# Convolution and GRU on one core: weights loaded first, the early convolution moved into step 1

## The chip, the core and the metric

One core of a Trainium2 chip runs the kernel. The time is device time in microseconds for one execution, the median of several runs. TensorE multiplies, VectorE, ScalarE and GpSimd do the elementwise work, SyncE only issues transfers; ScalarE and GpSimd issue some too. All engines run their own instruction lists and wait for each other through semaphores.

## What is computed

```python
# x (128, 64, 512), cond (128, 512), b (512), W_ih, W_hh (512, 1536), b_ih, b_hh (1536)
y = x + causal_depthwise_conv(x, taps=cond) + b      # 128 taps over 64 steps: lags 0 to 63 count
h = cond                                             # (batch 128, 512)
for t in range(64):
    gi, gh = y[:, t] @ W_ih + b_ih, h @ W_hh + b_hh
    r, z = sigmoid(gi_r + gh_r), sigmoid(gi_z + gh_z)
    n = tanh(gi_n + r * gh_n)
    h = (1 - z) * n + z * h
    out[:, t] = y[:, t] + h
```

## The kernel before

The batch has 128 rows, the channels four blocks of 128 (KB = 4). Every matrix product is made of three: each operand is split into a high part (rounded to fp32r) and a low part (the rest), and high x high, high x low and low x high are added in PSUM (block_product, L1077). A gate's product over the four channel blocks is thus 12 matmuls of 512 columns, and a step has six such groups: three gates of w_hh on h, three of w_ih on the convolved input of the next step, whose transposed form is xT.

The convolution is made in two parts. The **early** one gives steps 0 to 15 (EARLY = 16): x_early, a load of the first 16 inputs, times toep_early, the taps spread out by eight instructions (four on ScalarE, L655, four on VectorE, L862) from tap_blocks, which comes by way of the DRAM tensor tap_pad. It is 64 products into three PSUM banks (L1066 to L1075), whose 16 results VectorE evicts (L872) and SyncE stores to the DRAM tensor early, from which the xT of steps 1 to 15 are loaded (load_early_xT, L403). In the kernel before it is made before step 0. Step 0's own xT is made directly, from one row of x transposed on TensorE, times the tap of lag 0 plus the bias (L661 to L665).

The **late** (bulk) convolution gives steps 16 to 63: 128 banks of four matmuls (bulk, L1088), ten banks a step at ten points between the groups of steps 1 to 13 (POINTS, BULK_FIRST, BULK_LAST; bulk_bank, L325). Each needs a block of x_unit (loads of 256 KB in runs of 128 bytes, L418) split into high and low parts by ScalarE and VectorE (split), the taps' ring toep_ring (L429), and two evicting instructions (first_half on ScalarE, second_half on VectorE); the results go to the DRAM tensor xres, from which the xT of the later steps come.

From step FIRST_PAIR = 18 on, the w_ih products of two steps are made together with seven instead of eight half products (L1135, L1196 to L1258), with sums of inputs from GpSimd and combinations of the weights.

The order at the start is that of the instruction lists. SyncE (L372 to L407): tap_rows, h0, x_row, x_early, the twelve loads of w_ih, four biases broadcast to all partitions, then w_hh, then the stores of the early results, the xT of step 1, x_unit and toep_ring. ScalarE (L621 to L697): tap_pad, tap_blocks, bias_d and bias_pair issued, x_row reordered, k_full (the transposed taps), hT_hi, k_parts, its spread taps, xT of step 0, kernel_parts stored, the high parts of w_ih, the biases put into PSUM (put_bias), the high parts of w_hh. VectorE (L841 to L883): the low parts (low_weights, L352) in turns with the evictions, GpSimd those of the last channel block (on_pool). TensorE opens the PSUM banks of the gates with a matmul (L1053), makes the early convolution, then step 0.

## Time and profile before

| | us |
|---|---|
| median of 3 runs | 1177.78 (1176.2 to 1178.16) |
| profiled execution, its own time | 1179.38 |
| its span, first to last instruction | 1177.5 |
| TensorE busy (matmul) | 1135.4 (96%) |
| VectorE busy | 690.0 (59%) |
| ScalarE busy | 506.3 (43%) |
| GpSimd busy | 145.7 (12%) |

TensorE is busy in 96% of the span. It is the engine to follow: where it idles, the trace says which instruction of which engine released it. The page's slices show it idle in the first one above all. The other engines have room on average, but the average mixes stages: the start, steps with late convolution, and the paired steps.

### The profile page before, as it was taken

Reading aid. Unit: us, or ns where it says so; the run is one execution under the profiler, and the core shown is the slowest. Engines: PE = TensorE matmul, PEld = TensorE weight load, DVE = VectorE, ACT = ScalarE, POOL = GpSimd, SP = SyncE. Lnnn points to the kernel's source line nnn. Section 1 sums busy time; section 2 is a strip of 40 time slices with the busy share of each in tenths; the row PEclk is TensorE's granted clock in tenths of the full one; section 3 lists DMA queues with packets and bytes.
Section 4 is the critical chain, followed back from the end, with each engine's and each line's share of the span. In section 5 each row is a group of like instructions: output and inputs, shape, how many; then the busy total and the mean of one; then the engine's idle time right before and its main releaser. Section 6 shows DMA issues by size and latency. Waiting matters only on the chain.

```text
span 1177.5 us, 16672 instructions
## 1 busy us (share of the span) xinstructions
PE 1135.4 (96%) x5796; PEld 960.1 (82%) x5796; DVE 690.0 (59%) x1026; ACT 506.3 (43%) x965; POOL 145.7 (12%) x175
## 2 busy tenths in 40 slices
PE   1999999999999999999999999999999999999997
PEld 1977887878888888888888888888888888888885
DVE  2746775766775375555555655655555555655554
ACT  4527776767775343333323233333333333233332
POOL 0320010001001421111111000111111111100110
PEclk9999999999999999999999999999999999999999
DMA  9988888888863601110111111011111011111001
GB/s 247 286 193 167 160 172 165 173 174 171 174 151 91 147 18 37 36 35 25 31 36 36 36 36 28 25 36 36 36 36 27 27 36 36 36 36 32 26 23 27
DMA packets 284008, 96.97 MB, mean 82 GB/s; under 512 B 212688, under 2 KB 275664, under 8 KB 281920
## 3 DMA queue, kind: packets, MB, share of 16 engines
q1 hardware_dynamic: 278208, 91.83, 34.0%
q0 software_dynamic: 1664, 3.41, 0.9%
q10 hardware_dynamic: 4096, 1.22, 0.4%
q8 instruction: 23, 0.38, 0.1%
q14 instruction: 17, 0.14, 0.0%
HBM read 62.26 MB, written 34.14 MB: 82 GB/s over the span
## 4 chain that ended last, share of the span: by engine, by line
PE 92%; SPq 2%; ACT 1%; DMA 1%; DVE 1%; issue 1%; ACTq 0%; DVEq 0%
PE bank L1081 40%; PE sum_a L1140 17%; PE sum_c L1140 12%; PE bank L1174 7%; PE bank L1178 4%; PE sum_c L1081 3%; PE sum_a L1105 3%; PE bank L1043 2%; PE sum_a L1070 2%; PE sum_c L1105 1%; SPq L422 1%; PE sum_c L1070 1%; DMA early<-early_result 1%; SPq L435 1%; ACT toep_early L655 0%
## 5 line engine op out<-in xcount | busy, mean ns | idle before, releaser
L1081 PE MATMUL bank<-w_hh_hi,hT_hi 128*128 128x512 f32 x584 | 232.3, 398 | 0.1
L1081 PE MATMUL bank<-w_hh_lo,hT_hi 128*128 128x512 f32 x584 | 228.4, 391 | 0.0
L1081 PE MATMUL bank<-w_hh_hi,hT_lo 128*128 128x512 f32 x584 | 227.8, 390 | 0.0
L783 ACT ACTIVATE n_gate<-q 128x512 f32<-128x512 f32 x64 | 40.5, 633 | 249.2 <-DVE q L984 249.2
L1081 PEld LDWEIGHTS bank<-w_hh_hi,hT_lo 128*128 128x128 f32 x584 | 109.9, 188 | 23.9
L1081 PEld LDWEIGHTS bank<-w_hh_hi,hT_hi 128*128 128x128 f32 x584 | 109.9, 188 | 22.4 <-DVE hT_lo L838 0.5
L1081 PEld LDWEIGHTS bank<-w_hh_lo,hT_hi 128*128 128x128 f32 x584 | 110.3, 189 | 17.8
L823 ACT ACTIVATE hT_hi<-bank 128x512 fp32r<-128x512 f32 x63 | 37.6, 597 | 140.1 <-PE bank L1043 140.1
L838 DVE TENSOR_TENSOR hT_lo<-bank,hT_hi 128x512 fp32r<-128x512 f32 x64 | 44.1, 689 | 87.4 <-ACT hT_hi L823 87.0
L596 POOL TENSOR_TENSOR x_sum<-xT 128x256 f32<-128x256 f32 x23 | 17.3, 752 | 628.2 <-DMA xT<-xres 628.1
L889 DVE TENSOR_TENSOR x_parts<-x_unit,x_parts 128x512 fp32r<-128x512 f32 x64 | 70.5, 1102 | 39.0 <-ACT x_parts L706 38.8
L772 ACT ACTIVATE r<-bank 128x512 f32<-128x512 f32 x64 | 38.2, 597 | 119.2 <-PE bank L1178 113.0
L996 DVE TENSOR_TENSOR q<-z,q 128x512 f32<-128x512 f32 x64 | 45.4, 709 | 75.3 <-ACT z L802 74.9
L974 DVE TENSOR_TENSOR q<-bank,r 128x512 f32<-128x512 f32 x64 | 44.1, 688 | 63.5 <-PE bank L1081 62.2
L706 ACT ACTIVATE x_parts<-x_unit 128x512 fp32r<-128x512 f32 x64 | 73.7, 1152 | 17.5 <-PE sum_a L1105 8.2
L987 DVE TENSOR_TENSOR q<-h,n_gate 128x512 f32<-128x512 f32 x64 | 54.2, 847 | 35.7 <-ACT n_gate L783 35.7
L1174 PE MATMUL bank<-w_hh_hi,hT_hi 128*128 128x512 f32 x184 | 72.1, 392 | 0.8 <-ACT hT_hi L823 0.8
L1174 PE MATMUL bank<-w_hh_lo,hT_hi 128*128 128x512 f32 x184 | 71.6, 389 | 0.0
L716 ACT ACTIVATE tmp<-sum_a,bias_pair 96x128 f32<-96x128 f32 x172 | 52.0, 355 | 23.5 <-PE sum_a L1105 22.9
L551 POOL DMA_DIRECT2D out_dram<-outZ x52 | 28.4, 553 | 263.0 <-DVE outZ L1032 262.7
L1081 PE MATMUL bank<-w_ih_hi,xT_hi 128*128 128x512 f32 x144 | 60.1, 417 | 0.0
L1105 PEld LDWEIGHTS sum_a<-x_parts,toep_ring 128*96 128x96 f32 x344 | 44.9, 163 | 17.9 <-issue 5.3
(153 smaller groups left out, 2375.2 us busy)
## 6 DMA issues: line engine op xcount, KB each, us to landing
x_unit<-in_x_dram SPq DMA_DIRECT2D x64, 256.0 KB, 4.6
out_dram<-outZ SPq DMA_DIRECT2D x204, 64.0 KB, 1.6
toep_ring<-kernel_parts SPq DMA_DIRECT2D x128, 96.0 KB, 3.2
xres<-stage SPq DMA_DIRECT2D x32, 384.0 KB, 4.8
xT<-xres SPq DMA_DIRECT2D x192, 64.0 KB, 1.9
early<-early_result SPq DMA_DIRECT2D x4, 1024.0 KB, 13.6
xT<-early SPq DMA_DIRECT2D x60, 64.0 KB, 2.1
out_dram<-outZ POOLq DMA_DIRECT2D x52, 64.0 KB, 3.0
```

What stands on the lines that cost most here:

```text
L706: nc.scalar.activation(part_block(j, 0), x_block(j), ACT.Copy).then_inc(x_hi_ready, 1)
L716: nc.scalar.activation(tmp[m % 2][0:2 * LATE, pair * B:(pair + 1) * B], conv_bank[m % 3][0:2 * LATE, pair * 2 * B:pair * 2 * B + B], ACT.I ...
L838: nc.vector.tensor_tensor(lo_out[:, :], full[:, :], hi_in[:, :].bitcast(F32), ALU.subtract).then_inc(lo_ready, 1)
L889: nc.vector.tensor_tensor(part_block(j, 1), x_block(j), part_block(j, 0).bitcast(F32), ALU.subtract).then_inc(x_lo_ready, 1)
L974: nc.vector.tensor_tensor(q[:, :], ps_hn[:, :], r[:, :], ALU.mult).then_inc(reset_h_ready, 1)
L987: nc.vector.tensor_tensor(gate_in_order(q), in_order(h), gate_in_order(n_gate), ALU.subtract).then_inc(h_less_n_ready, 1)
L996: nc.vector.tensor_tensor(q[:, :], z[:, :], q[:, :], ALU.mult).then_inc(z_part_ready, 1)
L1081: mm = nc.tensor.matmul(psum[:, :], a[:, rows], b[w][:, cols], start=False, stop=stop and n == 2, skip_group_check=True)
L1105: mm = nc.tensor.matmul(conv_bank[m % 3][0:2 * LATE, pair * 2 * B:pair * 2 * B + cols], late, parts[j % HL_RING][:, slot * 2 * B:slot * 2 ...
L1140: mm = nc.tensor.matmul(total[:, at], stationary, cols, start=opens and k == 0 and n == 0, stop=k == 1 and n == 2, skip_group_check=True)
L1174: nc.tensor.matmul(ps_r[:, :], hT_hi[:, k * P:(k + 1) * P], part[1][:, w_cols(k, R)], start=False, stop=False, skip_group_check=True)
L1178: mm = nc.tensor.matmul(ps_r[:, :], hT_lo[:, k * P:(k + 1) * P], hi[1][:, w_cols(k, R)], start=False, stop=k == KB - 1, skip_group_check=True)
```

## The change

- POINTS is 12, and the late convolution uses 11 of them: 11 banks a step in steps 3 to 14 (BULK_OF).
- SyncE loads tap_rows, h0, then w_hh and w_ih. x_early (it lies where x_rows and the taps lie now) is loaded after everything that reads those is done. The early results go out in eight stores from three tiles.
- The early convolution is made in step 1, two banks at each of the points 2 to 9 (early_banks, early_products).
- x of steps 0 to 3 is made directly: x_rows, four loads from ScalarE's queue in runs of 128 bytes, 16 transposes on TensorE (transpose_x), the tap of lag 0 and the bias on ScalarE (y_base), the other lags by 24 multiply-adds of 128 columns on VectorE (y_sums). The loads from the DRAM tensor early begin with step 4.
- The biases are loaded as rows and brought into PSUM by four matmuls with a tile of ones; ScalarE copies them to SBUF.
- Four spread_taps move from ScalarE to GpSimd, between its low parts; VectorE's four stand between its low parts too. bias_d and bias_pair are issued by GpSimd.
- In step 0 TensorE makes the w_hh products first, each as its low parts come, then those of w_ih (first_step_products). The high parts' order is w_hh R, N, Z, w_ih R, N, Z.
- Pairs start at step 20 instead of 18; the loads and combinations around it move a step on.

The core of the diff:

```diff
-POINTS = 10
-BULK_FIRST, BULK_LAST = 1, 13
+POINTS = 12
+DIRECT = 4
+EARLY_STEP, EARLY_POINT = 1, 2
+BULK_FIRST, BULK_LAST = 3, 14
-    QUARTERS = 4
+    RESULTS = 8
+    RESULT_TILES = 3
-    FIRST_PAIR = EARLY + 2
+    FIRST_PAIR = EARLY + 4
...
-        GATES = ((R, Z, N), (R, N, Z))
-        W_PARTS = [(w, k, g) for w in range(2) for g in GATES[w] for k in range(KB)]
+        GATES = ((R, N, Z), (R, N, Z))
+        W_PARTS = [(w, k, g) for w in (1, 0) for g in GATES[w] for k in range(KB)]
...
+            load_weights(1, w_hh)
             load_weights(0, w_ih)
...
+            sp.wait_ge(tap_pad_stored, 16 * 2)
+            sp.wait_ge(k_parts_stored, 16 * QUADS)
...
+            sp.wait_ge(y_base_ready, KB * DIRECT)
+            sp.wait_ge(y_sum_ready, Y_SUMS[-1])
+            for b4 in range(4):
+                bs = slice(b4 * B // 4, (b4 + 1) * B // 4)
+                sp.dma_start(
+                    x_early[:, :].rearrange("p (b g) -> p b g", g=G0)[:, bs],
+                    x[bs, 0:EARLY, :].rearrange("b s (c g) -> (s c) b g", g=G0),
+                ).then_inc(x_early_loaded, 16)
...
+            for n in range(RESULTS):
+                sp.wait_ge(early_evicted, (n + 1) * NB0 // RESULTS)
...
+                sp.wait_ge(early_stored[n], 16 * len(range(n, RESULTS, RESULT_TILES)))
+            for t in (DIRECT, DIRECT + 1):
+                sp.wait_ge(outT_ready, t - RING + 1)
+                load_early_xT(t)
...
+                if isinstance(t, int) and t == BULK_LAST:
+                    store_stage(NBANK * 2 // STAGE - 1)
+                    for n in range(2):
+                        sp.wait_ge(stage_stored[n], 32 * (PAIRS // STAGE // 2))
+                    sp.wait_ge(outT_ready, BULK_LAST)
+                    for late in range(EARLY, BULK_LAST + RING):
+                        load_xT(late % RING, T - 1 - late)
...
+            for q4 in range(QUADS):
+                pool.dma_start(bias_d[q4 * QUAD:(q4 + 1) * QUAD, :],
...
+            low_parts(1, R)
+            pool.wait_ge(tap_blocks_loaded, 16)
+            pool.wait_ge(in_block_set, 1)
+            spread_taps(0)
+            low_parts(1, N)
+            spread_taps(1)
+            low_parts(1, Z)
+            spread_taps(2)
+            low_parts(0, R)
+            spread_taps(3)
+            low_parts(0, N)
+            low_parts(0, Z)
...
+            store_early_out(0)
+            pool.wait_ge(early_done, NB0)
+            nc.gpsimd.memset(toep_ring[:, :].bitcast(F32), 0.0).then_inc(toep_cleared, 1)
+
+            for t in range(1, BULK_LAST):
+                store_early_out(t)
...
+            act.dma_start(b_rows[0:1, :], b_ih.unsqueeze(0)).then_inc(bias_loaded, 16)
+            act.dma_start(b_rows[1:2, 0:N], b_hh[0:N].unsqueeze(0)).then_inc(bias_loaded, 16)
+            act.dma_start(b_hn_row[:, :], b_hh[N:NG].unsqueeze(0)).then_inc(bias_loaded, 16)
+            for k in range(KB):
+                act.dma_start(
+                    x_rows[:, k * D:(k + 1) * D].rearrange("b (t q r) -> b (t q) r", q=QUADS, r=QUAD),
+                    x[:, 0:DIRECT, :].rearrange("b t (q k r) -> b k (t q) r", q=QUADS, k=KB)[:, k],
+                ).then_inc(x_rows_loaded, 16)
...
+            act.wait_ge(banks_opened, 1)
+            for tile, psum in ((bias_rz[:, R:R + D], ps_r), (bias_hn[:, :], ps_hn), (bias_rz[:, Z:Z + D], ps_z),
+                               (bias_in[:, :], ps_in)):
+                nc.scalar.activation(tile, psum[:, :], ACT.Copy).then_inc(biases_kept, 1)
+            act.wait_ge(tap_pad_stored, 16 * 2)
+            act.dma_start(tap_blocks[:, :].rearrange("p (u g) -> p u g", g=G0),
+                          bass.AP(tap_pad.tensor, tap_pad.offset, [[G0, P], [D, EARLY], [1, G0]])
+                          ).then_inc(tap_blocks_loaded, 16)
...
+            def y_base(t):
+                act.wait_ge(x_rows_done, t + 1)
+                for k in range(KB):
+                    nc.scalar.activation(xT[t][:, k * P:(k + 1) * P], ps_x[t][:, k * P:(k + 1) * P], ACT.Identity,
+                                         bias=bias_d[:, k:k + 1],
+                                         scale=k_full[:, k * P + T - 1:k * P + T]).then_inc(y_base_ready, 1)
+
+            high_weights(1, R)
+            act.wait_ge(bias_early_done, 1)
+            nc.scalar.activation(bias_early[:, :], ps_hT[:, 0:G0], ACT.Copy).then_inc(bias_early_ready, 1)
+            high_weights(1, N)
+            act.wait_ge(conv_bias_loaded, 16 * (QUADS + 2))
+            y_base(0)
+            act.wait_ge(y_base_ready, KB)
+            nc.scalar.activation(xT_hi[:, :], xT[0][:, :], ACT.Copy).then_inc(xT_hi_ready, 1)
+            high_weights(1, Z)
+            y_base(1)
+            y_base(2)
+            high_weights(0, R)
+            y_base(3)
+            high_weights(0, N)
+            high_weights(0, Z)
...
+                if not isinstance(i, bass.RuntimeValue) and t == 0:
+                    act.wait_ge(y_sum_ready, Y_SUMS[1])
+                    nc.scalar.activation(xT_hi[:, :], xT[1][:, :], ACT.Copy).then_inc(xT_hi_ready, 1)
...
+            def y_sums(t):
+                for lag in range(1, t + 1):
+                    for k in range(KB):
+                        at = slice(k * P, (k + 1) * P)
+                        tap = k * P + T - 1 - lag
+                        nc.vector.scalar_tensor_tensor(xT[t][:, at], ps_x[t - lag][:, at], k_full[:, tap:tap + 1],
+                                                       xT[t][:, at], ALU.mult, ALU.add).then_inc(y_sum_ready, 1)
+            low_parts(1, R)
             dve.wait_ge(tap_blocks_loaded, 16)
+            spread_taps(4)
+            spread_taps(5)
+            low_parts(1, N)
             low_part(xT_lo, xT[0], xT_hi, xT_hi_ready, xT_lo_ready, 1)
+            spread_taps(6)
+            low_parts(1, Z)
+            y_sums(1)
+            spread_taps(7)
+            low_parts(0, R)
+            y_sums(2)
+            low_parts(0, N)
+            y_sums(3)
+            low_parts(0, Z)
...
+            pe.wait_ge(bias_loaded, 16 * 3)
+            pe.wait_ge(ones_set, 1)
+            for psum, rows, bias in ((ps_r, 2, b_rows[0:2, R:R + D]), (ps_z, 2, b_rows[0:2, Z:Z + D]),
+                                     (ps_in, 1, b_rows[0:1, N:NG]), (ps_hn, 1, b_hn_row[:, :])):
+                mm = nc.tensor.matmul(psum[:, :], ones[0:rows, :], bias, start=True, stop=True)
+            mm.then_inc(banks_opened, 1)
...
+            def early_products(n):
+                if n >= 3:
             ...
+                for slot in range(BANK // B):
+                    g = n * (BANK // B) + slot
+                    mm = nc.tensor.matmul(conv_bank[n % 3][:, slot * B:(slot + 1) * B],
+                                          toep_early[:, g * P:(g + 1) * P],
+                                          x_early[:, :].rearrange("p (b g) -> p g b", g=G0)[:, g, :],
+                                          start=True, stop=True)
+                mm.then_inc(early_done, 1)
...
+            def first_step_products():
+                for psum, gate in ((ps_r, R), (ps_hn, N), (ps_z, Z)):
+                    for k in range(KB):
+                        low_weights_ready(1, k, gate)
+                        block_product(psum, hT_hi, hT_lo, 1, gate, k, False)
+                    if gate == R:
+                        pe.wait_ge(x_rows_loaded, 16 * KB)
+                        for t in range(DIRECT - 1):
+                            transpose_x(t)
+                        pe.wait_ge(bias_early_ready, 1)
+                        transpose_x(DIRECT - 1)
+                pe.wait_ge(xT_lo_ready, 1)
+                for psum, gate, done in ((ps_r, R, gh_r_done), (ps_in, N, gh_n_done), (ps_z, Z, gh_z_done)):
+                    for k in range(KB):
+                        low_weights_ready(0, k, gate)
+                        mm = block_product(psum, xT_hi, xT_lo, 0, gate, k, k == KB - 1)
+                    mm.then_inc(done, 1)
...
+                            for n in early_banks(t, g * POINTS // GROUPS):
+                                early_products(n)
```

## Rows read from the trace of the kernel before

**Rows 1.** The page, first part: busy time, share, instructions of each engine
```profile
PE 1135.4 (96%) x5796; PEld 960.1 (82%) x5796; DVE 690.0 (59%) x1026; ACT 506.3 (43%) x965; POOL 145.7 (12%) x175
```
**Rows 2.** Stretches: length, busy time of PE, PEld, DVE, ACT, POOL, clock, DMA share, GB/s
```profile
0.00:29.50 29.50, 4.54 (x14) 3.11 (x15) 6.10 (x10) 11.86 (x15) 2.08 (x11) 1.00 0.94 247
...
29.50:82.70 53.20, 53.19 (x240) 47.43 (x241) 32.92 (x44) 22.12 (x39) 14.71 (x8) 1.00 0.96 247
82.70:105.00 22.30, 18.68 (x96) 14.34 (x95) 11.65 (x19) 14.06 (x28) 2.32 (x4) 1.00 0.83 159
...
105.00:368.00 263.00, 257.84 (x1387) 215.87 (x1386) 178.35 (x288) 188.99 (x408) 26.11 (x48) 0.99 0.78 163
```
**Rows 3.** TensorE's waits, 105 to 380 us: total, times, longest
```profile
PE sum_c L1105 <- issue: 2.7, 2, 1.9
```
**Rows 4.** The chain that ended last, by start and length, 0 to 130 us
```profile
9.67 2.96 ACTq L631
```
**Rows 5.** TensorE in order of time, 28 to 112 us: the first product after the convolution
```profile
57.55 0.59 PE L1081 MATMUL bank<-w_ih_hi,xT_hi 128*128 128x512 f32 x1
```
**Rows 6.** Stretches with weights' loads alone, and with x_unit's alone
```profile
30.00:35.00 5.00, 5.00 (x25) 4.86 (x24) 3.27 (x5) 3.79 (x9) 0.00 (x0) 1.00 1.07 229
...
70.00:74.00 4.00, 4.00 (x19) 3.34 (x18) 2.01 (x3) 3.04 (x5) 0.00 (x0) 1.00 1.08 172
```
**Rows 7.** SyncE's issues of two tiles: nanoseconds min/median/max, first and last start
```profile
L385 SPq DMA_DIRECT2D w_ih_raw<-in_L_cond_W_ih_dram x12: 426/432/4763, 16.2 to 25.8; - x12
...
L422 SPq DMA_DIRECT2D x_unit<-in_x_dram x64: 617/1258/2707, 67.8 to 321.0; - x64
```
**Rows 8.** ScalarE in order of time: table load, xT pieces, high parts
```profile
15.12 1.28 ACT L640 ACT_TABLE_LOAD   x1 [15.12 <-issue]
...
27.92 1.45 ACT L662 ACTIVATE xT<-sum_c,bias_d,k_full 128x128 f32<-128x128 f32 x4
...
46.41 2.18 ACT L683 ACTIVATE w_hh_hi<-w_hh_raw 128x512 fp32r<-128x512 f32 x4
```
**Rows 9.** DMA issues, 0 to 110 us: count, KB each, median us to landing
```profile
tap_blocks<-tap_pad ACTq DMA_DIRECT2D x1, 512.0 KB, 5.2
...
kernel_parts<-k_parts ACTq DMA_DIRECT2D x4, 128.0 KB, 10.0
```
**Rows 10.** DMA queues (q1 SyncE's, q10 ScalarE's), 12:14 us, then 36:41: packets, MB, share
```profile
q10 hardware_dynamic: 1967, 0.50, 110.2%
q1 hardware_dynamic: 99, 0.10, 16.4%
...
q1 hardware_dynamic: 593, 1.54, 77.3%
q10 hardware_dynamic: 526, 0.47, 27.5%
```
**Rows 11.** Spread taps, GpSimd's 1024-column add, and VectorE's low parts of w_ih
```profile
18.78 3.89 DVE L862 TENSOR_SCALAR toep_early<-tap_blocks,in_block 128x1024 f32<-128x1024 f32 x4
...
41.90 2.38 POOL L540 TENSOR_TENSOR bias_rz<-bias_rz,bias_tmp 128x1024 f32<-128x1024 f32 x1 [38.89 <-DMA bias_hn<-in_L_cond_b_hh_dram]
...
L354 DVE TENSOR_TENSOR w_ih_lo<-w_ih_raw,w_ih_hi x9: 681/682/2067, 32.2 to 50.0; 128x512 fp32r<-128x512 f32 x9
```
**Rows 12.** Chain rows of 512-column matmuls at both levels; a stretch with its clock
```profile
18.21 0.86 PE bank L1054 x2
...
382.65 2.73 PE sum_c L1081 x12
...
184.00:188.00 4.00, 4.00 (x18) 3.42 (x17) 1.88 (x4) 2.52 (x6) 0.00 (x0) 0.71 0.85 172
```
**Rows 13.** VectorE's transposes that end steps 19 and 63
```profile
475.22 0.71 DVE L1032 STREAM_TRANSPOSE outZ<-outT 128x512 f32<-128x512 f32 x1
...
1173.19 0.71 DVE L1032 STREAM_TRANSPOSE outZ<-outT 128x512 f32<-128x512 f32 x1
```
**Rows 14.** GpSimd's stores of step 3's output: four issues, and the pause before
```profile
152.72 2.17 POOL L551 DMA_DIRECT2D out_dram<-outZ  x4 [19.15 <-DVE outZ L1032]
```

More of the change, by code:

```diff
@@ L136, in conv_residual_gru @@
     toep_early = place("toep_early", G0 * P)
-    quarter = [None] * QUARTERS
-    for n in reversed(range(QUARTERS)):
-        quarter[n] = place(f"early_result{n}", G0 // QUARTERS * B)
-    assert top[0] <= gru_end
+    result = [place(f"early_result{n}", G0 // RESULTS * B) for n in range(RESULT_TILES)]
+    assert top[0] <= outT_at
     top[0] = x_at
@@ L171, in conv_residual_gru @@
     lag0_row = place("lag0_row", 8, parts=EARLY)
-    bias_tmp = place("bias_tmp", N)
-    assert top[0] <= w_at["hh"] + KB * NG * KW
-    top[0] = w_at["hh"] + KB * NG * KW
-    x_row, h0 = place("x_row", D), place("h0", D)
+    h0 = place("h0", D)
+    ones = place("ones", P, parts=2)
+    b_hn_row = place("b_hn_row", D, parts=1)
+    assert top[0] <= toep_at
+    top[0] = bias_first_at
+    b_rows = place("b_rows", NG, parts=2)
+    assert top[0] <= bias_first_at + 2 * NCOL * KW
+    top[0] = outZ_at
+    tap_blocks = place("tap_blocks", EARLY * G0)
+    assert top[0] <= outZ_at + 2 * D * KW
     ctx = ExitStack()
@@ L183, in conv_residual_gru @@
         ps_in = sum_c[:, BANK:2 * BANK]
-        ps_x0 = conv_bank[2]
+        ps_x = [*conv_bank, ps_hT]
         def sem(name):
@@ L767, in step @@
                 first_half(bulk_bank(t, 0))
-                if not isinstance(i, bass.RuntimeValue) and t == 0:
-                    for n in range(QUARTERS):
-                        act.wait_ge(early_stored[n], 16)
                 act.wait_ge(gh_r_done, t + 1)
@@ L945, in step @@
                     x_first_low(0, u + 1)
-                    for n in range(2, NCOMBO):
-                        combo_low(n)
                 if odd and follows:
@@ L993, in step @@
                     sums_low(slice(D, 2 * D), sum34_hi_ready, sum34_lo_ready, j + 1)
+                if not isinstance(i, bass.RuntimeValue) and t == 0:
+                    low_part(xT_lo, xT[1], xT_hi, xT_hi_ready, xT_lo_ready, 2)
+                split(split_block(t, 4))
+                second_half(bulk_bank(t, 4))
+                early_evicts(t, 4)
                 dve.wait_ge(h_less_n_ready, t + 1)
@@ L1052, in _, with transpose_x @@
+            mm.then_inc(banks_opened, 1)
+            def transpose_x(t):
+                for k in range(KB):
+                    mm = nc.tensor.transpose(ps_x[t][:, k * P:(k + 1) * P],
+                                             x_rows[:, k * D + t * P:k * D + (t + 1) * P], ident[:, :])
+                mm.then_inc(x_rows_done, 1)
             pe.wait_ge(hT_hi_ready, 1)
-            for psum in (ps_r, ps_z, ps_in, ps_hn):
-                mm = nc.tensor.matmul(psum[:, :], hT_hi[:, 0:P], hT_hi[:, :], start=True, stop=True)
```

320 lines of the change are left out of this document (140 added, 180 removed).

## The prediction

> **What bounds the kernel now.** The shares of the span come first: TensorE is busy for 1135.4 of 1177.5 us, so only the 42 us in which it is not, and the work that it is given, can move the time [rows 1]. Then the stretches: TensorE idles 25.0 us of the first 29.5, then runs to 82.7 us without a gap (early convolution, all gates of step 0, w_ih products of step 1); it idles 3.6 us to 105 us, while the late convolution starts, and 5.2 us from there to 368 us [rows 2]. The waits put these last down to "issue" at the late convolution's matmuls, 1.9 us the longest [rows 3]. The chain of waits shows what fills the first 29 us: ScalarE's queue is stuck for 2.96 us issuing behind a transfer [rows 4], and its spread taps and the pieces of xT follow.
>
> So the sum is made on TensorE: when its continuous work starts, how far the first step stretches, and what is lost later. Its reference is the start of step 1 at 82.7 us plus the 3.6 us lost in that step, 86.3 us, with the early convolution done. In the new kernel that convolution, the 28.0 us from 29.5 to 57.55 [rows 5], falls into step 1.
>
> **ScalarE's queue up to the first weights (T0).** Three bias rows at 0.43 us, as the issue of any unblocked load [rows 7], from 0.8 us on give 2.1 us. The four x_rows loads have 2048 runs of 128 bytes each, as x_unit's loads have. Those move 172 GB/s, 1.5 us for 256 KB, and hold their issuer for a median 1.26 us; a weights' load, over 32 partitions, gets 229 GB/s, 1.14 us for 256 KB [rows 6, 7]. SyncE now issues 24 of those from 1.7 us on. If the two queues take turns, four x_rows loads take 4 x (1.5 + 1.14) = 10.6 us, and ScalarE is stuck behind them as it was behind tap_blocks: free at 13, after three small issues at 14.2 us (9 if nothing blocks, 17 if more weights slip in). Table load 1.3, k_full, hT_hi and k_parts three at 0.5, four bias copies at 0.55: 19.2 us [rows 8]. The four openings by a row of ones, now plain f32, have no row; the nearest are the old ones at 0.43 us each [rows 12]. Even at four times that they end by 13 us and cost nothing; without that cover, up to 7 us. Then tap_blocks' issue 0.4, the block behind it 3.0, kernel_parts' four 1.7: T0 = 24.3 us, between 18.5 and 32.
>
> **tap_blocks' landing (L).** It used to have no weights ahead of it and landed in 5.2 us; kernel_parts, 512 packets issued among weights' loads, took 10.0 us [rows 9]. While both hardware queues had work, at 36 to 41 us, they moved 593 and 526 packets: one for one, whatever their size [rows 10]. Taken one for one with weights' packets, tap_blocks' 2048 would land only once all weights have: 24 x 1.14 + 4 x 1.5 + 1.8 for tap_blocks + 4 for start and landing = 39 us. So L is between 19 (issued at 14 us, if nothing blocks, and 5.2 on) and 39. I take 31: 10.0 us from 19.5 would be 29.5, and this has four times the packets.
> The Trainium skill (DMA: Bandwidth & Descriptors, "Queues, rings and completion order") says that each DMA engine goes round the queues that hold work, packet by packet. The equal counts of [rows 10] agree with it. By that rule alone L would be 39.
>
> **The first step's products (their end, F).** ScalarE: 24 high parts at 0.55 = 13.1, sixteen pieces of xT at 0.33 = 5.2, xT_hi and bias_early 0.9 [rows 8]: 19.3 us, and with 3.7 for the last low part and products T0 + 23. GpSimd: its four spread_taps have no row, and lie between VectorE's 1.0 and twice its own 2.38 for a 1024-column add, to which I set them; with six low parts at 1.2, half of it, that is 17 us and up [rows 11], beside ScalarE's. VectorE's order puts spread_taps(4) ahead of all but the first low parts, so from L on it owes four spreads 4.0, fifteen low parts at 0.68 = 10.2, xT_lo 0.7, and 24 adds of 128 columns. Those have no row; between a quarter of VectorE's 0.68 and ScalarE's 0.36 for that size I take 0.23: 5.5 us. That is 20.4, and 0.3 of the last product: 20.7. GpSimd works beside it, and low parts that did so went up to 2.07 us [rows 11]; I add 2 (0 to 6). F is the larger of 24.3 + 23 = 47.3 and 31 + 20.7 + 2 = 53.7: **53.7 us**, between 41.5 and 65. VectorE becomes the bound, behind a late transfer. The low parts used to be hidden by the early convolution; they stand bare now.
>
> **Clock.** TensorE works in bursts in that step. After a long pause two 512-column matmuls took 0.86 us, where twelve take 2.73: 0.43 and 0.23 each, the 1.2 and the 2.4 GHz level; after 1.7 us of waiting at 180 us the granted clock fell to 0.71 [rows 12]. A gate's group of 2.7 us would take 5.2, over a pitch of 3.5 to 4. From 0 to 4 us; I take 0, since VectorE is the later one.
>
> **The turn of the step.** After F come q's add, tanh, a bias copy, the xT_hi of step 1 and its xT_lo: 0.7 + 0.6 + 0.6 + 0.6 + 0.7, some 3.3 us of idle TensorE. Then x_r and x_n 5.4, transposes 0.4, x_z 2.7: step 1 begins at F + 11.9 = 65.6 us and, with 28.0 us of convolution, stands at 93.6 where the old kernel stood at 86.3: **+7.3 us**. The x_early load waits for the last adds (F - 2) and moves 4.19 MB, 17 us at the first stretch's 247 GB/s [rows 2], less as it then runs alone; it is wanted six groups of 0.68 us into step 1, at F + 16. That is 0 to 1 us, I take 0; past that cover each us costs one. The 16 evictions lie beside 44 us of TensorE.
>
> **Pairs.** FIRST_PAIR goes from 18 to 20, so one pair of steps is made directly: 2 x (6 x 2.73 + 0.4) = 33.6 us [rows 12] against 2 x (1173.19 - 475.22) / 44 = 31.7 us [rows 13]: **+1.9 us**.
>
> **Late convolution.** 128 banks go from 13 steps of ten to 12 of eleven; TensorE's work is the same. A step of ten took 19.15 + 2.17 = 21.3 us [rows 14], 4.5 more than one without. Eleven will take 21.75 us, 1.98 a bank for 2.13, so its DMA share of 0.78 [rows 2] becomes 0.84. The stalls of 5.2 us at a bank can grow with it, and the 3.6 us at the start can recur in step 3. 0 to 5 us more; I take **+2.3**. The combined low parts after h move one step on, where TensorE has products of w_ih to cover them. GpSimd's six loads at the start, some 0.55 us each [rows 14], delay k_zeroed to about 7 us; ScalarE wants it at 15. The 12 added transposes, 1.3 us, fit into TensorE's gaps. The xT loads of steps 16 and 17 go ahead of the store and have 8 us of cover.
>
> **Sum.** 7.3 + 1.9 + 2.3 = +11.5 us. The profiled execution took 1179.38 us around its span of 1177.5, 1.6 above the median 1177.78: 1190.9 against itself, **1189.3** against the median.
>
> **Rivals.**
> *Starved queue*: weights win the packets, L = 39, F = 61.7: 8 us more, 1197 us; with VectorE slowed fully 1201. For it: the one-for-one counts. Against: at 12 to 14 us tap_blocks moved 1967 packets to the other queue's 99 [rows 10], so that queue could run dry while tap_blocks was taken in.
> *Free queues* (the other side): the x_rows issues don't block ScalarE, which is free at 9 us; T0 = 18.5, L = 19 to 21, F = 41.5 to 44.5. Step 1 stands 4.9 to 1.9 us ahead, and with the pair's 1.9 that is 1174.8 to 1177.8; if the late convolution, begun two steps later, loses half of its 8.8 us less, down to 1170. It decides at F = 44.5: below that, faster. For it: w_ih's loads were issued at 0.43 us, faster than they moved. Against: x_unit's 1.26.
> *The late convolution binds*: eight more waits of 2 us, 16 in place of 2.3: 1203 us. For it: waits of up to 1.9 us at ten banks a step. Against: only some five in 128 banks.
>
> **How the numbers follow.** Forecast 0.47 (its own range 1182 to 1195), starved 0.17, late convolution 0.08, free 0.28. Of the last, 0.18 lies more than 0.2% below (2.4 us, about what a measurement here can tell) and 0.10 within it; slower is 0.72. The range leaves out the far ends of the free and the late-convolution case: 1174 to 1202.
>
> **What would show it.** ScalarE's first high part of w_hh at 24 us (18.5: free; over 30: starved). tap_blocks landing at 31 with VectorE's spread right behind. Step 0's last w_ih product ending at 54, TensorE idle for 3 us after it, step 1 from 66 us on for 45 us. Over 14 us of waits at late banks would prove the third rival. The prediction is wrong at the root if TensorE's products in step 0 follow each other without gaps, or if x_early is what step 1 waits for.

## The result, and the profile after

The changed kernel takes **1225.8 us** (median of 4 runs, 1222.0 to 1226.9) where the kernel before, run beside it, takes 1177.0: a ratio of 1.041 (1.038 to 1.044), 48.8 us more. Forecast were 1189.3 us, 1174 to 1202. The direction was right, and two of the three terms of the sum were far too small. The profiled execution has a span of 1223.5 us, against 1177.5 before: +46.0 us, and this is what is split up below. One of e3's four runs took 1270.6 us at a granted clock of 0.85, where the others took 1192.7 to 1193.5 at 0.99; it is left out of e3's numbers.

The page of the changed kernel, its busy line (answers to [rows 1]):

```profile
PE 1154.9 (94%) x5800; PEld 965.5 (79%) x5800; DVE 694.8 (57%) x1041; ACT 500.8 (41%) x971; POOL 159.1 (13%) x185
```

TensorE is 19.5 us longer busy: its four openings by a row of ones take 7.6 us where the old ones took 2.4, twelve transposes and a directly made pair of steps came in, and more of its products run at the 1.2 GHz level (below: *cold* products). Its idle time grew from 42 to 69 us. The stretches say where (columns as in [rows 2]; the first two are that group's, the others follow the new kernel's course):

```profile
0.00:29.50 29.50, 8.21 (x12) 3.20 (x12) 1.10 (x3) 0.00 (x0) 5.94 (x18) 1.00 1.02 213
29.50:82.70 53.20, 31.88 (x115) 23.11 (x116) 33.39 (x56) 29.26 (x59) 26.13 (x10) 0.94 0.45 110
41.50:75.70 34.20, 25.58 (x88) 17.98 (x88) 30.12 (x50) 22.66 (x48) 26.13 (x10) 0.90 0.18 51
86.00:130.00 44.00, 44.00 (x202) 39.46 (x201) 16.08 (x24) 5.28 (x9) 4.34 (x5) 1.00 0.25 96
165.00:420.00 255.00, 239.78 (x1284) 196.96 (x1283) 167.89 (x274) 180.52 (x392) 24.05 (x44) 0.99 0.80 167
```

In the first stretch the DMA share is 1.02 and ScalarE (0.00) computes nothing at all. Where the old kernel filled 29.5 to 82.7 us with TensorE (53.19 of 53.20), the new one has 31.9 us of it and the DMA engines stand at 0.45. Step 1 with the early convolution (86 to 130 us) runs without a gap, as forecast. In the late part (165 to 420 us) 15.2 us of 255 are idle, at a DMA share of 0.80.

The chain that ended last, 0 to 78 us, by start, length and what:

```profile
1.88 0.41 ACTq L682
2.32 2.78 ACTq L682
5.13 9.92 ACTq L682
15.08 14.76 ACTq L682
29.88 5.41 ACTq L687
...
41.54 0.64 ACT w_hh_hi L722
42.20 0.70 DVE w_hh_lo L374
43.04 5.15 PE bank L1180 x12
48.20 0.45 PE sum_a L1147 x4
48.73 1.52 ACT xT L727 x4
50.27 0.64 ACT xT_hi L738
50.94 0.69 DVE xT_lo L889
51.63 1.88 DVE toep_early L911
53.52 1.72 DVE w_hh_lo L374 x3
...
62.30 3.15 DVE w_ih_lo L374 x3
...
70.55 5.09 PE bank L1180 x12
75.65 0.64 ACT xT_hi L855
```

ACTq L682 are the four x_rows issues: for 27.96 us ScalarE gets no further in its instruction list. L687 is tap_pad behind them. So T0, ScalarE's first w_hh high part, is 41.5 us and not 24.3. Behind it is a chain through four engines in turn: a low part, twelve products at the 1.2 GHz level (5.15 us; [rows 12] has 2.73 for twelve at 2.4), the transposes of x, ScalarE's pieces, and then VectorE without a pause from 50.9 to 70.5 us, and twelve cold products again (5.09 us). The end of step 0's products, F, is 75.6 us where 53.7 was forecast.

The DMA queues between 2 and 20 us (as in [rows 10]; q1 is SyncE's, q10 ScalarE's):

```profile
q1 hardware_dynamic: 1925, 3.50, 85.8%
q10 hardware_dynamic: 3129, 0.40, 18.3%
```

x_rows has 8192 packets of 128 bytes. In 18 us 3129 of ScalarE's went through, for 1925 of the weights', and the weights had the engines for 86% of the time. Both queues made progress, packet beside packet if not exactly one for one, but a packet of x_rows carries a sixteenth of what one of the weights' does. The last x_rows load landed at 36.7 us, the last of the weights at 35.0.

TensorE's waits from 130 to 420 us (total, times, longest), against [rows 3]:

```profile
PE sum_a L1204 <- issue: 8.0, 6, 2.2
PE sum_c L1204 <- issue: 5.3, 3, 2.5
PE sum_a L1204 <- DVE stage L986: 3.7, 4, 1.2
```

All are at products of late banks, 17.0 us; the third rival was to be proved by 14.

### The profile page after: what moved, and what is told of

Its sections match the earlier page's. It is cut to its first block, busy times and chain, and to the rows that moved or that the text cites. A ratio compares the mean times of both kernels' runs of the same rounds, so it can differ in the third digit from the quotient of the medians.

```text
span 1223.5 us, 16696 instructions
## 1 busy us (share of the span) xinstructions
PE 1154.9 (94%) x5800; PEld 965.5 (79%) x5800; DVE 694.8 (57%) x1041; ACT 500.8 (41%) x971; POOL 159.1 (13%) x185
## 3 DMA queue, kind: packets, MB, share of 16 engines
q1 hardware_dynamic: 275760, 88.95, 31.9%
## 4 chain that ended last, share of the span: by engine, by line
PE 83%; DVE 5%; ACT 4%; ACTq 3%; issue 2%; SPq 2%; DMA 0%; DVEq 0%
PE bank L1180 36%; PE sum_a L1251 15%; PE sum_c L1251 11%; PE bank L1289 7%; PE sum_c L1180 3%; PE bank L1293 3%; ACTq L682 2%; PE bank L1132 2%; PE sum_a L1204 2%; PE sum_a L1170 2%; ACT x_parts L754 2%; SPq L446 1%; PE sum_c L1204 1%; DVE x_parts L972 1%; ACT tmp L764 1%
## 5 line engine op out<-in xcount | busy, mean ns | idle before, releaser
L1180 PE MATMUL bank<-w_hh_hi,hT_lo 128*128 128x512 f32 x592 | 232.2, 392 | 0.0
L1180 PE MATMUL bank<-w_ih_hi,xT_hi 128*128 128x512 f32 x160 | 68.1, 426 | 4.3 <-POOL w_ih_lo L374 1.7
L1180 PE MATMUL bank<-w_ih_hi,xT_lo 128*128 128x512 f32 x160 | 63.4, 396 | 0.0
```

Source lines behind the costliest of these rows:

```text
L1180: mm = nc.tensor.matmul(psum[:, :], a[:, rows], b[w][:, cols], start=False, stop=stop and n == 2, skip_group_check=True)
```

## The experiments

Times in us. L is where tap_blocks landed (issue plus its time to landing), F the end of step 0's products, "x_unit" the start of the first and of the last x_unit load, ratio that to the kernel before with its 95% interval.

| kernel | T0 | L | F | x_unit | time | ratio |
|---|---|---|---|---|---|---|
| before | - | - | - | 67.8, 321.0 | 1177.0 | 1 |
| changed | 41.5 | 41.8 | 75.6 | 129.0, 380.3 | 1225.8 | 1.041 (1.038 to 1.044) |
| e1 | 27.1 | 38.6 | 69.1 | 122.5, 372.8 | 1213.8 | 1.030 (1.023 to 1.036) |
| e2 | 29.6 | 37.7 | 69.2 | 122.5, 374.2 | 1218.8 | 1.034 (1.030 to 1.038) |
| e8 | 24.0 | 24.3 | 58.4 | 111.7, 364.6 | 1209.1 | 1.027 (1.025 to 1.029) |
| e9 | 24.2 | 24.5 | 55.9 | 113.5, 365.1 | 1210.2 | 1.028 (1.026 to 1.030) |
| e12 | 23.5 | 23.8 | 56.9 | 112.4, 365.6 | 1210.1 | 1.027 (1.024 to 1.030) |
| e13 | 23.9 | 24.1 | 54.5 | 109.8, 359.5 | 1204.9 | 1.024 (1.022 to 1.025) |
| e3 | - | - | - | 67.2, 316.1 | 1193.0 | 1.012 (1.009 to 1.016) |
| e14 | - | - | - | 68.4, 327.9 | 1174.9 | 0.998 (0.997 to 0.999) |

e1, e2, e8, e12 and e13 have two runs each. Those of e1 lie 10.7 us apart (1208.4 and 1219.1), the others 1.6 to 2.5, so that a difference of 1 or 2 us between two of these kernels says nothing. e8 contains the edit of e2; e9 and e12 contain e8, and e13 contains e12.

**The start: what holds ScalarE, and tap_blocks.**

```diff
+            sp.wait_ge(x_rows_loaded, 16 * KB)
             load_weights(1, w_hh)
```

> The changed kernel, with one wait added on SyncE: the 24 weights' loads begin only when the four x_rows loads have landed. Theory A (ScalarE's queue is held up because its x_rows loads share the DMA engines with the weights): alone, the four loads of 256 KB in 128-byte runs need some 1.5 us each, ScalarE is past them by about 10 us instead of 29.8, its first w_hh high part comes at 18 to 20 us instead of 41.5, and the time falls by 15 to 20 us, to about 1208. Rival (the x_rows loads are slow of themselves, 7 us each for 2048 runs, weights or no weights): ScalarE is still stuck until about 28 us, the weights land 20 us later than before, the first high part stays at 40 us or later and the time is 1226 or more. Theory B (the chain from that high part to the end of the first step's products takes 34 us of itself): that distance stays 34 us in both cases.

ScalarE in order of time, 1 to 28 us (start, length, line, what):

```profile
1.88 5.68 ACTq L683 DMA_DIRECT2D x_rows<-in_x_dram  x4
...
13.42 0.43 ACTq L705 DMA_DIRECT2D tap_blocks<-tap_pad  x1
13.89 9.80 ACTq L710 DMA_DIRECT2D kernel_parts<-k_parts  x1
...
27.13 2.19 ACT L723 ACTIVATE w_hh_hi<-w_hh_raw 128x512 fp32r<-128x512 f32 x4 [11.65 <-issue]
```

Theory A holds for the cause and missed the sizes: alone, the four issues take 5.7 us, beside the weights 28. T0 came at 27.1, not 18 to 20, because the block moved on: one kernel_parts issue now stood 9.8 us behind tap_blocks, and tap_blocks, issued 25 us earlier than in the changed kernel, landed only 3 us earlier:

```profile
tap_blocks<-tap_pad ACTq DMA_DIRECT2D x1, 512.0 KB, 25.1
```

It landed at 38.6 us, while the last four of the 24 weights' loads were still under way (42.4 us for the last). Theory B failed here and in e2: from T0 to F it is 42.0 and 39.6 us, not 34, as VectorE now waits for tap_blocks; counted from L it is 30.5 and 31.5 us (33.8 in the changed kernel).

```diff
-                act.dma_start(x_rows[:, k * D:(k + 1) * D]..., x[:, 0:DIRECT, :]...)   # 128-byte runs
+                act.dma_start(x_plain[:, t * D:(t + 1) * D], x[:, t, :])               # 2 KB runs
```

> The changed kernel, with x of steps 0 to 3 loaded as four loads of whole 2 KB rows (512 runs in all in place of 8192) and put into the order of x_rows by four VectorE copies, some 0.7 us each. The weights still go out at the same time. If the two queues are served run for run (theory A in its strict form), 512 runs are through after as many of the weights' runs, and ScalarE is free by about 5 us: first w_hh high part at 19 us or when the weights have landed (w_hh r landed within 10 us), time about 1226 - 22 = 1204. Rival (the share goes by bytes, or the issue order does it, and the size of the runs does not matter): ScalarE free at 15 us or later, first high part at 27 us or more, time 1211 or more. Theory B: the chain from the first high part to the end of the step's products stays at 34 us.

```profile
1.88 1.81 ACTq L684 DMA_DIRECT2D x_plain<-in_x_dram  x4
...
14.04 1.28 ACT L692 ACT_TABLE_LOAD   x1 [14.04 <-POOL k_parts L574]
...
15.97 0.40 ACTq L703 DMA_DIRECT2D tap_blocks<-tap_pad  x1
...
17.29 8.98 ACTq L708 DMA_DIRECT2D kernel_parts<-k_parts  x1
```

With the same bytes in 512 packets the four issues take 1.81 us, so it is the number of packets that held the queue. ScalarE was free by 6.2 us and then waited until 14.0 for GpSimd's k_parts, which stood behind a bias_pair issue that came 7.1 us late (2.6 in e1, where the weights had not yet been issued): this, the weights' own landing and kernel_parts' issue put T0 at 29.6 and not 19, and the time at 1218.8 and not 1204. tap_blocks landed at 37.7 us, 21.7 us after its issue. The Trainium skill (DMA: Bandwidth & Descriptors, "Queues, rings and completion order") says that each DMA engine goes round the queues with work packet by packet. e2 agrees: tap_blocks landed 0.2 us behind the last of the weights (37.5 us), near the 39 us that the prediction had for turns of one to one; the counts above, 3129 to 1925, say that the turns are not exactly that.

```diff
             load_weights(1, w_hh)
+            sp.wait_ge(tap_blocks_loaded, 16)
             load_weights(0, w_ih)
```

> The kernel e2_x_rows_contiguous with one wait added: SyncE issues w_ih's twelve loads only when tap_blocks has landed. In e2 tap_blocks was issued at 15.9 us and landed 21.7 us later, at 37.7 us, with the last of the weights. Theory A' (tap_blocks' 2048 packets wait among the weights' packets): it now shares with the last of w_hh alone and lands 5 to 8 us after its issue, by 24 us; VectorE's spreads begin 13 us earlier, step 0's products end at 24 + 31 = 55 us in place of about 69, and the time falls by 10 to 14 us, to about 1206. It costs nothing unless w_ih, landed by 38 us, comes after ScalarE wants it. Rival (tap_blocks is slow of itself, its 128-byte runs out of a buffer just written): it lands after 38 us again, w_ih after 50 us, and the time is over 1230.

tap_blocks, 2048 packets of 256 bytes, landed 8.2 us after its issue, at 24.3 us, and F came at 58.4 for 69.2 (55 was expected): theory A' holds, and w_ih came in time. F gained 10.8 us, and the time 9.7, just under the 10 to 14 expected. Of the 48.8 us that the change costs, the two edits of e2 and e8 give back 17.

**The chain from T0 to F.** It took 34.1 us in the changed kernel, 34.4 in e8, where tap_blocks lands 0.3 us after T0 and so no longer holds it up.

```diff
-            spread_taps(0..3) on GpSimd, between its low parts
+            the same four on VectorE, behind low_parts(0, Z)
```

> The kernel e8_tap_blocks_before_w_ih with GpSimd's four spread_taps (4.4 to 5.1 us each in the changed kernel) made by VectorE behind its last low part. They are wanted in step 1 only. Theory B (GpSimd's spreads delay its own low parts, and slow VectorE's work beside them: two spreads took 2.9 us, three low parts 3.6): VectorE's spreads go to 1.0 us and its low parts to 0.68, TensorE waits for no low part of GpSimd, and the first step's products end 22 to 25 us after tap_blocks' landing in place of 31; time 5 to 8 us below e8, some 1199. A share of it can be lost at the start of step 1, as x_early's load, 12.2 us long, now goes out only after those four spreads. Rival (the chain is set by ScalarE's 24 high parts and 16 pieces and by TensorE's 1.2 GHz stretches): it stays at 29 us or more and the time within 2 us of e8.

F fell by 2.5 us, to 31 us behind L and not 22 to 25, and the time not at all. Theory B's numbers failed and the rival's came true, in part for another reason than the rival's: the spreads were wanted "in step 1 only", but they stood in VectorE's instruction list ahead of q, which the next step's input waits for, and TensorE waited 4.4 us for xT_lo behind them:

```profile
60.30 0.80 PE L1183 MATMUL bank<-w_ih_hi,xT_hi 128*128 128x512 f32 x1 [4.36 <-DVE xT_lo L883]
```

```diff
             def first_step_products():
+                transpose_x(0..2)
                 for psum, gate in ((ps_r, R), (ps_hn, N), (ps_z, Z)):
                     ...
-                    if gate == R: transpose_x(0..2)
```

> The kernel e8_tap_blocks_before_w_ih with TensorE's transposes of x of steps 0 to 2 put ahead of the first w_hh products, in place of behind the r gate's twelve. In e8 ScalarE stood waiting for them until 31.4 us, behind a group of products at 1.2 GHz (5.35 us), and VectorE for xT_lo from 32.1 to 33.6 us, with 20.7 us of its own work still to do. Theory (that detour is on the chain to the end of the first step): xT_lo comes about 2 us earlier, the end of step 0's products at 56 us in place of 58.4, and the time falls by 2 us, to 1207. Rival (ScalarE's order of high parts sets it): less than 0.7 us.

xT_lo came 2.0 us earlier (31.6 us), F 1.5 us, and the time stayed, so the theory failed on the time. The traces show where the 1.5 us went. Here are the twelve products behind F, then the next twelve, first in e8, then in e12:

```profile
59.81 3.01 PE bank L1186 x12
62.83 2.73 PE sum_c L1186 x12
```
```profile
58.91 4.34 PE bank L1186 x12
63.25 2.98 PE sum_c L1186 x12
```

e12 starts them 0.9 us earlier and ends them 0.7 us later, since they run at a granted clock of 0.77 (58.9 to 66.3 us) and those of e8 at 1.00. VectorE in e12, from 31.6 us on:

```profile
31.61 0.68 DVE L889 TENSOR_TENSOR xT_lo<-xT,xT_hi 128x512 fp32r<-128x512 f32 x1
...
39.24 3.76 DVE L376 TENSOR_TENSOR w_ih_lo<-w_ih_raw,w_ih_hi 128x512 fp32r<-128x512 f32 x3
...
52.12 2.98 DVE L376 TENSOR_TENSOR w_ih_lo<-w_ih_raw,w_ih_hi 128x512 fp32r<-128x512 f32 x3
```

Three low parts take 1.89 us when GpSimd is quiet (the last row below); in e12 it works all through, and they take up to 3.76. The last kernel of this line puts GpSimd's four spreads on ScalarE, behind its last high part:

```diff
             high_weights(0, Z)
+            for c in range(C0 // 2): nc.scalar.activation(toep_early_block(c), ..., scale=in_block[:, c:c + 1])
```

> The kernel e12_transposes_first with GpSimd's four spread_taps made by ScalarE behind its last high part, where it stood idle from 43.7 to 47.8 us; the old kernel paid 1.85 us for one there. In e12 VectorE worked without a pause from 31.6 to 54.9 us, 23.3 us, and in e9, where GpSimd had no spreads, the same work took 19.7 us; but e9 put four spreads of 0.96 us into VectorE's own queue behind it. Theory B (GpSimd's spreads slow VectorE's low parts beside them and hold back its own; e9 gave the gain back by its four spreads): VectorE's stretch is 19.7 us, step 0's products end at 53 to 54 us in place of 56.9, x_early's load goes out 3 us sooner, and the time falls by 3 us, to about 1206.5. Rival (the time of the changed kernel no longer hangs on the end of step 0, as the late convolution's supply takes the gain): under 1 us.

```profile
39.38 1.87 DVE L376 TENSOR_TENSOR w_ih_lo<-w_ih_raw,w_ih_hi 128x512 fp32r<-128x512 f32 x3
...
49.17 1.89 DVE L376 TENSOR_TENSOR w_ih_lo<-w_ih_raw,w_ih_hi 128x512 fp32r<-128x512 f32 x3
```

VectorE's stretch is 18.9 us (32.2 to 51.1) in place of 23.5, F 54.5 for 56.9, the time 5.2 us below e12: theory B holds, and 2 us more came than it said (the late part took 274.9 us from first to last product in place of 278; why, was not tried). What GpSimd's spreads cost VectorE is thus 4.6 us; what its low parts cost is still in the 18.9. The rest of the chain is the detour by the cold group and ScalarE, of which e12 took 2 us, and the cold group at its end, which no run took away.

e13 also shows what a good start alone is worth. Its step 1 begins at 66.7 us, where the prediction had 65.6, and still it takes 1204.9 us and not 1189.3. Of the 15.6 us between them 14.5 are lost behind that point.

**The late convolution.**

```diff
-POINTS = 10
-BULK_FIRST, BULK_LAST = 1, 13
+POINTS = 12
+BULK_FIRST, BULK_LAST = 1, 12
```

> The kernel before with one thing changed: the late convolution's 128 banks are spread over steps 1 to 12 with eleven a step, in place of steps 1 to 13 with ten. TensorE has the same products in all. Theory C (the late banks are bounded at about 2.18 us each by what feeds them, whatever stands around them): eleven banks make a step of 24.0 us, the last bank comes at the same time as before, but by then TensorE has done about 1.2 steps less of the gates, so the time grows by 12 to 18 us, to 1190 to 1195. Rival (the late part in the changed kernel was slow through its late start, not through eleven banks a step): a step takes 22.6 us and the time stays within 3 us of 1177.

The kernel before becomes 14.5 us slower (10 to 19) by this alone. Its start is untouched. From the first x_unit load to the last it is 248.9 us, and from the first late product to the last 276.1 us; in the changed kernel 276.3, in e13 274.9. That is 2.16 us a bank, whatever the start. Theory C holds.

```diff
             def load_x_part(unit, part):
+                if unit >= 2: return
```

> The changed kernel without the x_unit loads of units 2 to 7 (12.6 of 16.8 MB of x): the late convolution multiplies the first two units' x again and again. This leaves part of the loading out, so the output is not the reference's. Theory C1 (the supply of the late banks through the DMA engines and SyncE's queue is the bound, at 2.18 us a bank): steps 3 to 13 fall from 24.1 to the 22.6 us or less of TensorE's work, TensorE's idle time of 15 us between 165 and 420 us mostly goes, and the time falls by 13 to 17 us to about 1210. Rival C2 (the splits and evictions on ScalarE and VectorE, one bank behind, hold the banks): steps 3 to 13 stay at 24 us and the time at 1224 to 1226.

One run, 1205.0 us, with a span 20.7 us below the changed kernel's. Its stretch and TensorE's only waits from 105 to 400 us:

```profile
165.00:420.00 255.00, 254.42 (x1380) 212.49 (x1379) 176.21 (x289) 186.79 (x411) 26.85 (x48) 1.00 0.52 124
```
```profile
PE sum_a L1206 <- DVE stage L988: 1.1, 2, 0.9
```

ScalarE and VectorE still have all their splits and evictions, and TensorE is idle for 0.6 us. So it is the transfers (C1), not the crowding (C2). Not all that they cost shows as a wait. Here are the changed kernel and e4 from the first late product to the last, with the same 1386 products of TensorE:

```profile
149.00:425.50 276.50, 259.07 (x1386) 212.45 (x1386) 180.46 (x294) 194.37 (x422) 25.32 (x47) 0.99 0.79 163
```
```profile
149.90:405.00 255.10, 253.38 (x1386) 211.10 (x1386) 179.94 (x294) 193.00 (x423) 25.18 (x47) 1.00 0.54 127
```

Of the 21.4 us between them 15.7 are idle time; in 5.7 the same products take longer, in part because they are cold after a wait (granted clock 0.99 for 1.00). In e3 it is likewise: 16.5 us of waits at late banks for 8.6 in the kernel before, and TensorE busy for 1141.5 us in place of 1135.4.

GpSimd's stores show the length of a step of eleven without and with x_unit's traffic; the first fence is e4, the second the changed kernel:

```profile
218.00 2.17 POOL L603 DMA_DIRECT2D out_dram<-outZ  x4 [19.91 <-DVE outZ L1123]
239.85 2.17 POOL L603 DMA_DIRECT2D out_dram<-outZ  x4 [19.68 <-DVE outZ L1123]
```
```profile
196.21 2.19 POOL L601 DMA_DIRECT2D out_dram<-outZ  x4 [19.45 <-DVE outZ L1121]
222.22 2.18 POOL L601 DMA_DIRECT2D out_dram<-outZ  x4 [23.81 <-DVE outZ L1121]
```

21.9 us against 26.0 here, 24.2 in the mean of eleven steps (from the store at 148.1 us to that at 414.5). The 21.75 us of the prediction were TensorE's own time and right; they were not what counted.

Is it SyncE's single queue or the DMA engines behind it?

```diff
-                    load_toep(m // 2 + 3)        # SyncE
+                        load_toep_here(m // 2 + 3)   # GpSimd, as are the first ones
```

> The changed kernel with all loads of toep_ring issued by GpSimd, whose queue then holds them and the early outputs; SyncE keeps x_unit, xT and the stores of stage. From SyncE's first x_unit load to its last it is 253.2 us in the kernel before, 251.3 in the changed one, 248.9 with eleven banks a step: the late convolution takes 250 us however it is spread. Theory C1a (SyncE's single queue, in which each load is held up behind the one before it, sets that 250 us; the DMA engines are busy only 0.80 of the time): with the small loads in a queue of their own it falls to 240 us or less, TensorE's idle 15 us between 165 and 420 us mostly goes, and the time falls by 8 to 14 us, to about 1214. Rival C1b (the DMA engines' own work on 128-byte runs sets it): it stays at 250 us and the time within 3 us of 1226. Rival C1c (GpSimd issues a toep load more slowly than SyncE's 1 us and stands in the way of its own): longer than 253 us, time over 1230.

> The kernel before with the same edit: all loads of toep_ring issued by GpSimd. TensorE stands idle 5.2 us between 105 and 350 us there, and 3.6 us in step 1. Theory C1a: the waits at late banks go, 3 to 7 us less, some 1172. Rival C1b: within 2 us of 1177.5. Rival C1c: 5 us or more slower.

Both fell to the third case, and far beyond its number. e11 takes 1366.9 us (1.161, 1.158 to 1.164); e10's two timings lie far apart (1423.6 and 2918.1), its span is 1421.3. GpSimd's waits in e11, 105 to 540 us:

```profile
POOL toep_ring L549 <- issue: 317.5, 112, 5.7
```

An issue is 0.69 us, but the next one follows only some 3 us later, with nothing in the profile that it waits for. Why is not shown. So this told nothing on SyncE's queue against the DMA engines: that stays open.

The kernel before the other way round: 128 banks in steps 1 to 14, nine a step and ten in two, first combined pair at step 20.

```diff
-POINTS = 10
-BULK_FIRST, BULK_LAST = 1, 13
+POINTS = 11
+BULK_FIRST, BULK_LAST = 1, 14
+        TEN = (12, 13)
```

> The kernel before with its 128 late banks in steps 1 to 14, nine a step and ten in two of them, in place of ten in steps 1 to 13; the first combined pair is step 20, as in the changed kernel. It goes the other way from e3_eleven_banks. Theory C (the late convolution takes 249 to 253 us from the first x_unit load to the last, however it is spread; what counts is how much of the gates' work TensorE has to fill them): TensorE's idle 8.8 us at late banks mostly goes, the later pair costs 0.7 (e7), and the time falls by 3 to 8 us, to 1170 to 1174. Rival (the idle time belongs to single banks wherever they stand, and eleven a step was slow through the crowding of ScalarE and VectorE): within 1.5 us of 1178.

```profile
105.00:350.00 245.00, 244.47 (x1313) 205.35 (x1312) 163.96 (x264) 173.06 (x370) 26.10 (x48) 1.00 0.80 166
```

Idle time in that stretch falls from 5.2 us in the kernel before to 0.5, and the time by 2.8 us (1.5 to 4.1): **1174.9 us, with e15 the fastest kernel of this study**, a little less than the 3 to 8 us of theory C. With room in the transfers it is TensorE that sets the pace: 259.5 us from the first x_unit load to the last.

**Single parts of the change on the kernel before.** FIRST_PAIR at 20 alone:

> The kernel before with FIRST_PAIR at 20 in place of 18, so that one pair of steps more is made directly. From the rows of the kernel before, a direct pair takes 33.6 us and a combined one 31.7: the theory gives +1.9 us, 1179. Rival (the combined products of the first pair had waits of their own, or the stretch behind them was cold): nothing, within 0.5 us.

1178.2 us, 1.0009 (0.9999 to 1.0020): +1.1 us, -0.1 to +2.4, which holds the 1.9 and does not prove it. The six bias loads on GpSimd alone:

> The kernel before with one part of the change alone: the six loads of bias_d and bias_pair are issued by GpSimd, in place of ScalarE. Before, ScalarE issues them behind tap_blocks' load and is held there until 12.6 us. Theory (ScalarE's queue at the start is on the path to the early convolution at 29.5 us): ScalarE is free some 3 us sooner, and the time falls by 1 to 3 us, to 1175 to 1176. Rival (x_early's 4.19 MB or the weights' landing sets the start of the early convolution): within 0.5 us of the kernel before.

1176.8 us, 0.9993 (0.9983 to 1.0004): nothing. The early convolution did start 4.4 us sooner (25.1 us for 29.5). But the last store of the early results took 12.25 us in place of 7.16, TensorE waited 3.3 us for the biases behind it, and the first x_unit load went out at 68.4 for 67.8. Then both together with e14:

> The kernel e14_late_banks_in_14_steps with the six bias loads on GpSimd, as in e6_bias_loads_on_gpsimd. In e6 the early convolution began 4.4 us sooner and nothing was left of it: the first x_unit load went out at 68.4 us for 67.8. Theory C (with TensorE's own work the bound in the late part, a gain at the start is kept as far as the gates of steps 0 and 1 allow): 1 to 3 us below e14. Rival (the gain is lost before that, in step 0, where TensorE waited 3.3 us for the biases): within 0.5 us of e14.

1175.1 us, 0.9981 (0.9972 to 0.9990), as e14. The early convolution starts at 26.1 us for e14's 30.0, and the rival was right: the gain is gone before step 1, and x_unit starts at 68.2 us again.

## Why the prediction failed, by its own steps

The span grew by 46.0 us. To the end of step 1 it is F + 10.2 + 28.0 - 86.3 = +27.6 where +7.3 stood; the pairs +1.1 where +1.9 stood; the late convolution +14.5 by e3 where +2.3 stood. That is 43 of 46. Of the 3 us left, 2.2 are idle time between 130 and 165 us, where the late convolution starts: the loss at its start, 3.6 us in the kernel before, came again in step 3, as the prediction had allowed.

- **ScalarE's queue (T0 24.3, measured 41.5): failed.** "If the two queues take turns, four x_rows loads take 4 x (1.5 + 1.14)" counts turns load by load. [rows 10] showed turns packet by packet, and the prediction used that for tap_blocks in the next paragraph, not here. The 8192 packets of x_rows meet all of the weights', so the loads are through only when nearly all weights are: 24 x 1.14 = 27 us for those and 6 for themselves gives 33; measured, the issues end at 29.8 and tap_pad behind them at 35.3. Alone they need 5.7 us (e1), as 512 packets 1.8 us (e2).
- **tap_blocks' landing (L 31, measured 41.8): failed**, twice over. In the changed kernel it was issued only at 38.2 and took 3.7 us, since the weights were in. Issued early it lands among or behind the last weights, at 38.6 and 37.7 us (e1, e2). The starved rival's 39 was the right end; "10.0 us from 19.5" was kernel_parts' own price, which has a quarter of the packets. L cost 10.8 us of the 20.3 us missed.
- **The first step's products (22.7 us behind L, measured 33.8): failed.** VectorE could not work off its queue from L on: it had to wait for xT_lo, behind cold products, the transposes and ScalarE, until 50.9 us; GpSimd's spreads were 4.4 to 5.1 us each, not 2.4; and beside GpSimd's spreads VectorE lost 4.6 us (e12 against e13), inside the 0 to 6 that stood. Counted on VectorE, the 11.1 us missed are 2.2 in which it was still at the first low parts when tap_blocks landed, 1.3 idle for xT_lo, 4.0 more work (a spread 1.7 us in the mean in place of 1.0, an add 0.28 in place of 0.23), and 3.6 at the end, where not one product but a cold group of twelve stands behind its low part.
- **Clock (0, measured 2.4 us at either end): failed.** "VectorE is the later one" was taken for cover. But the group of twelve after VectorE's last low part is bare: 5.09 us for 2.73. The stretch 41.5 to 75.7 us has a granted clock of 0.90. (The 2.4 us at the end are part of the 3.6 above.)
- **The turn (11.9, measured 10.2: 1.7 us too long), step 1 with the early convolution and x_early's cover: right.** Step 1's products begin at 85.85 us, 86 to 130 us is full, and no wait at x_early.
- **Pairs (+1.9): not contradicted** (e7).
- **The late convolution (+2.3, measured +14.5 to 17): failed**, and it is the third rival, at 0.08, that came true. The step held that eleven banks would take TensorE's 21.75 us and the DMA share would rise from 0.78 to 0.84. Its base, 21.3 us for a step of ten [rows 14], is a step without a wait: ten of them in a row, from the store at 131.4 us to that at 352.5, took 22.1 us each. The share came to 0.80: the transfers already gave all they could, 2.16 us a bank. "Only some five waits in 128 banks" was the evidence against; but with ten a step TensorE needs 21.4 us (between the 20.9 of e14's nine and 21.9 of e4's eleven), or 2.14 a bank. The two limits lay 1% apart, so few waits said nothing about the room behind them. With eleven TensorE needs 1.99 and the difference, 0.17 x 128 = 22 us less what ten already lost (8.8), gives 13. The rival priced it as 16 us of waits; the waits grew by 8.2 us (17.0 for 8.8), and in e3 by 7.9, where the same products taking 6.1 us longer make up the rest of the span's 13.7. What limits the supply, SyncE's queue or the DMA engines, stays open.
- **Chances.** The starved queue and the late convolution both happened, beside a chain that was 11 us too short; each was priced as a case by itself. Together they would have been 1189.3 + 8 + 14 = 1211, and even that leaves out ScalarE's own 28 us. Neither of the two signs of being wrong at the root came: TensorE's products in step 0 had gaps (8.6 us between 41.5 and 75.7), and x_early was not waited for.

## What to carry to other kernels

When two queues load at once, compare packets, not bytes or loads. Here 1 MB in 8192 packets of 128 bytes was through only when 6 MB of weights in packets of 2 KB were (36.7 and 35.0 us), and the engine that had issued it stood for 28 us. So put nothing with small packets beside a bulk load if an engine behind that queue is wanted. And before packing more work on a supplied stage, take the supply's time per piece by itself (first load to last): a stage with few waits can be at its limit, as this one was (2.14 us of TensorE's work and 2.16 of supply a bank), and there spreading wider (e14, -2.8 us) gains and spreading denser (e3, +14.5 us) loses.

## What was not expected of the hardware

- Four loads of 256 KB in 128-byte packets hold the issuing engine's queue for 5.7 us alone, 28 us beside the weights; in 2 KB packets 1.8 us beside the same weights.
- GpSimd's queue is held too: its second bias_pair issue came 7.1 us late in e2, beside the weights, and 2.6 in e1, ahead of them. And of 96 KB loads with 192-byte runs it gives out one in some 3.5 us (0.69 and a pause of 2.8), where SyncE had 128 of them and x_unit's 64 loads through in 253 us.
- GpSimd's product of 128x1024 with a column is 4.4 to 5.1 us beside a busy VectorE, twice its add of the same size; VectorE's own takes 0.97 [rows 11].
- VectorE's subtraction of 128x512 goes from 0.68 to 1.75 us when one of GpSimd's (1.27 us) lies beside it; beside GpSimd's spreads most take 0.68 us and some 1.52. The Trainium skill (SBUF — State Buffer, "SBUF: two separate sides") says that a VectorE instruction with two SBUF inputs and a GpSimd instruction that reads SBUF lock each other out for a whole instruction. The 1.75 us agree with that for GpSimd's low parts; beside the spreads of 4.4 to 5.1 us VectorE was never held that long, so there the trace does not agree.
